# Audio tower, one core: search, token lists and first expert weights drawn into the shared network's loop

## What is computed

```python
scores = jax.nn.softmax(flat_x @ gate_w.T, axis=-1).T
topk_weight, topk_idx = jax.lax.top_k(scores, C)       # C = 752 of 6016, for each of 16 experts
xg = flat_x[topk_idx]
g = jnp.einsum('ecd,eid->eci', xg, Wg)
u = jnp.einsum('ecd,eid->eci', xg, Wu)
h = jax.nn.gelu(g, approximate=False) * u
eo = jnp.einsum('eci,edi->ecd', h, Wd) * topk_weight[..., None]
flat_out = jnp.zeros_like(flat_x).at[topk_idx.reshape(-1)].add(eo.reshape(-1, d))
shared = jax.nn.gelu(hidden @ Sg.T, approximate=False) * (hidden @ Su.T) @ Sd.T
return flat_out + shared
```

## Time and profile before

| | us |
|---|---|
| median of 3 runs | 1786.75 (1784.9 to 1788.12) |
| the profiled execution | 1787.73 |
| its span, first to last instruction | 1785.9 |
| PE busy | 1650.1 (92%) |
| DVE, ACT, POOL busy | 1217.0, 933.1, 1018.6 |
| mean granted clock of PE | 0.961 of full speed |

### The profile page before, as it was taken

The page is one execution under the profiler, slowest core; times in us unless marked ns, Lnnn a source line. Parts: engine busy times, 40 slices in busy tenths (PEclk is TensorE's granted clock), DMA queues, the critical chain, the costliest instruction groups (busy, mean ns, idle before and its releaser), DMA issues.

```text
span 1785.9 us, 47094 instructions
## 1 busy us (share of the span) xinstructions
PE 1650.1 (92%) x15406; PEld 1235.7 (69%) x15406; DVE 1217.0 (68%) x3822; ACT 933.1 (52%) x2157; POOL 1018.6 (57%) x1073
## 2 busy tenths in 40 slices
PE   5983999999999995799998599999999999999997
PEld 5882666777777763577777377777777777777775
DVE  3884889999999995757786555555555555555541
ACT  3553777777777763442335444444444444444432
POOL 3772356666666655722241346676666666666665
PEclk9895999999999997899998699999999999999999
DMA  5542555566666652421001524443333344343322
GB/s 185 162 136 47 122 141 142 141 151 151 151 149 151 145 137 61 129 54 35 28 27 29 176 88 106 107 103 103 100 102 99 87 104 100 88 104 84 99 33 30
DMA packets 173651, 186.81 MB, mean 105 GB/s; under 512 B 119544, under 2 KB 146680, under 8 KB 167416
## 3 DMA queue, kind: packets, MB, share of 16 engines
q1 hardware_dynamic: 138488, 135.03, 26.9%
q0 software_dynamic: 35072, 50.62, 13.9%
HBM read 134.59 MB, written 50.44 MB: 104 GB/s over the span
## 4 chain that ended last, share of the span: by engine, by line
PE 55%; DVE 2%; ACT 1%; DMA 1%; issue 1%; POOL 0%; POOLq 0%; SPq 0%; DVEq 0%
PE psum L1757 28%; PE psum L1774 14%; PE psum L1622 6%; PE psum L1642 4%; PE psum L1737 1%; DMA arena<-e_u 1%; PE psum L1612 0%; PE psum L1682 0%; DVE arena L1228 0%; ACT arena L759 0%; DVE arena L399 0%; PE psum L1653 0%; DVE arena L1173 0%; DVE arena L1306 0%; PE psum L1708 0%
## 5 line engine op out<-in xcount | busy, mean ns | idle before, releaser
L658 POOL TENSOR_TENSOR arena<-arena 128x376 f16<-128x376 f32 x320 | 314.2, 984 | 359.2 <-ACT arena L759 357.7
L1757 PE MATMUL psum<-arena,hidden 128*128 128x376 f16 x3072 | 494.5, 324 | 0.9 <-DVE arena L1370 0.9
L1757 PEld LDWEIGHTS psum<-arena,hidden 128*128 128x128 f16 x3072 | 301.3, 98 | 189.9 <-issue 3.1
L759 ACT ACTIVATE arena<-arena 128x376 f16<-128x376 f32 (+5 forms) x610 | 284.2, 474 | 61.2 <-DVE arena L1306 45.5
L977 ACT ACTIVATE arena<-psum 128x376 f32<-128x376 f32 x256 | 123.7, 483 | 343.6 <-PE psum L1757 343.6
L1133 DVE CUSTOM_DVE_ANT_0 arena<-psum,constants 128x188 f32<-128x188 f32 x768 | 237.3, 346 | 51.4 <-PE psum L1449 41.3
L1380 DVE SCALAR_TENSOR_TENSOR arena<-psum,arena 128x376 f32<-128x376 f32 x256 | 140.6, 549 | 181.0 <-ACT arena L977 179.3
L1774 PE MATMUL psum<-hidden,arena 128*128 128x256 f16 (+1 forms) x2304 | 256.6, 273 | 0.0
L759 ACT ACTIVATE arena<-psum 128x188 f32<-128x188 f32 (+7 forms) x457 | 176.3, 397 | 147.3 <-PE psum L1737 58.0
L1774 PEld LDWEIGHTS psum<-hidden,arena 128*128 128x128 f16 (+1 forms) x2304 | 229.9, 103 | 21.7
L808 ACT ACTIVATE arena<-psum 128x376 f32<-128x376 f32 x384 | 183.8, 480 | 80.5 <-PE psum L1463 78.1
(11 more groups left out here) (159 smaller groups left out, 2736.0 us busy)
## 6 DMA issues: line engine op xcount, KB each, us to landing
arena<-e_g SPq DMA_DIRECT2D x16, 1024.0 KB
arena<-e_u SPq DMA_DIRECT2D x16, 1024.0 KB, 5.0
arena<-e_d SPq DMA_DIRECT2D x16, 1024.0 KB
arena<-x_t SPq DMA_DIRECT2D x32, 376.0 KB, 3.4
weighed<-arena POOLq DMA_DIRECT2D x32, 376.0 KB, 3.9
arena<-q_halves SPq DMA_DIRECT2D x192, 47.0 KB, 3.0
arena<-k_halves SPq DMA_DIRECT2D x96, 94.0 KB, 2.3
arena<-q_halves SPq DMA_DIRECT2D x96, 94.0 KB, 2.2
```

The lines of the kernel that those rows point to most:

```text
L658: nc.gpsimd.tensor_tensor(dst, f, hi, ALU.subtract).then_inc(ready, 1)
L759: return nc.scalar.activation(dst, src, ACT.Copy, scale=scale)
L1757: last = mm(bank[2 * (s % 2) + i][:, 0:CHUNK], w_, a, start=n == 0, stop=n == 5)
```

## The change

It has five parts.

1. The six pieces of work between `above_threshold` and the first `hot_part` stand in steps 45 to 48, not 45 to 51. `HOT` becomes 49, so each `hot_part` stands three steps earlier; 15 of the 16 are in the loop (12 before).
2. `hot_quarter(0)` stands at step 57 and `hot_quarter(1)` at step 61, in the loop. Quarters 2 and 3 stand behind it.
3. At step 62 DVE runs `tokens_of_slots(0)` and lists expert 0 (`FIRST_LISTED`). POOL's gathers of expert 0 wait for this list and stand behind its last low part of the loop. Expert 0's rows lie at another place (`XG[0]`), and their transposes go to PSUM banks 4 and 5.
4. Gate and up weights of expert 0 are loaded in the loop (three transfers at step 40, into the memory of the attention's weights, and one at step 50 into that of the scores). ACT casts them in steps 41 to 46, 51 and 52, twice each: to the fp16 high part, and in place, times 64, in fp32. POOL subtracts the two in steps 50 to 57 (`low_first`, eight subtractions of 128x512).
5. The down weights of expert 0 are cast and subtracted within `expert(0)`: four casts more in ACT's steps 2 to 5, four subtractions more in DVE's steps 3 to 6. `tokens_of_slots(1)` stands behind DVE's product of its step 0, `list_half(1, ...)` in its steps 1 and 2.

```diff
-HOT = FIRST + ROUNDS + 8
+HOT = FIRST + ROUNDS + 5
+FIRST_LISTED = HOT + 13
+LOADS = 40
...
-        XG = [Place(4136)(SLOT_TILES * ROW), at6(SLOT_TILES * ROW)]
+        XG = [Place(prep + 1288)(SLOT_TILES * ROW), at6(SLOT_TILES * ROW)]
...
+        W0 = [v[:, 0:W_GATE].bitcast(F32) for v in (WH, WL)]
+        FIRST_ST = [W0[p // 3][:, p % 3 * 512:(p % 3 + 1) * 512] for p in range(6)] + [PSC[:, p * 512:(p + 1) * 512] for p in range(2)]
...
+        def token_bank(e, c):
+            return bank[(4 if isinstance(e, int) and e == 0 else 6) + c]
...
+                if s == LOADS:
+                    sp.wait_ge(y_added, B)
+                    sp.dma_start(W0[0], e_g[0, :, 0:1536]).then_inc(w_first_in, 16)
+                    sp.dma_start(W0[1][:, 0:512], e_g[0, :, 1536:2048]).then_inc(w_in[0], 16)
+                    sp.dma_start(W0[1][:, 512:1536], e_u[0, :, 0:1024]).then_inc(w_first_in, 16)
+                if s == HOT + 1:
+                    sp.wait_ge(slots, 18)
+                    sp.dma_start(PSC, e_u[0, :, 1024:2048]).then_inc(w_in[1], 16)
...
-            load(0, 0)
             for par in range(2):
                 sp.wait_ge(sh_out[par], 32 * (KS // 2))
-            load(0, 1)
             load(0, 2)
...
+            def low_first(p):
+
+                i, h = divmod(p, 4)
+                pool.wait_ge(sh_added, 2 * 11)
+                pool.wait_ge(wh_ready[i], 2 * h + 2)
+                c = slice(512 * p, 512 * p + 512)
+                nc.gpsimd.tensor_tensor(WEL[0][:, c], FIRST_ST[p], WEH[0][:, c], ALU.subtract).then_inc(wl_ready[i], 1)
...
+                if HOT + 1 <= s < HOT + 9:
+                    low_first(s - HOT - 1)
...
             pool.wait_ge(hl_ready, STEPS)
+            pool.sem_inc(ehl_ready, RING)
+            pool.wait_ge(idx_listed, 4)
             clear_gathered(0)
-            pool.sem_inc(ehl_ready, RING)
             pool.wait_ge(xg_set, 1)
-            pool.wait_ge(idx_listed, 4)
...
+            first_steps = [LOADS + 1 + p for p in range(6)] + [HOT + 2, HOT + 3]
+
+            def high_first(p):
...
+                copy(WEH[0][:, 512 * p:512 * p + 512], FIRST_ST[p], WSCALE).then_inc(wh_ready[i], 1)
+                copy(FIRST_ST[p], FIRST_ST[p], WSCALE).then_inc(wh_ready[i], 1)
...
+                if s in first_steps:
+                    high_first(first_steps.index(s))
                 if s >= HOT + 4:
                     values_of_slots((s - HOT) // 4 - 1, (s - HOT) % 4)
...
+                    if first and 2 <= s < 6:
+                        high_weights(0, 2, s - 2, 0)
...
                 if s == done + 1:
                     above_threshold()
+                    step.mark(nc.vector.tensor_tensor_scan(RANK, ONE, EQ, 0.0, ALU.mult, ALU.add))
                 if s == done + 2:
-                    step.mark(nc.vector.tensor_tensor_scan(RANK, ONE, EQ, 0.0, ALU.mult, ALU.add))
+                    first_of_equal()
+                    ranks_of_hits()
                 if s == done + 3:
-                    first_of_equal()
+                    slots_of_hits()
                 if s == done + 4:
-                    ranks_of_hits()
-                if s == done + 5:
-                    slots_of_hits()
-                if s == done + 6:
                     whole_slots()
-                if s == done + 7:
                     parts_of_slots()
                 if s >= HOT:
                     hot_part(s - HOT)
+                if s == FIRST_LISTED:
+                    tokens_of_slots(0)
+                    list_half(0, (0,))
+            for n in range(STEPS - HOT, 4 * E // QE):
+                hot_part(n)
             down_out(KS - 2, 1)
...
+                    if first and s == 0:
+                        tokens_of_slots(1)
+                    if first and s in (1, 2):
+                        list_half(1, (2 * s - 2, 2 * s - 1))
+                    if first and 3 <= s < 7:
+                        low_expert(0, 2, s - 3, 0)
...
-                if s == done + 5:
+                if s == done + 3:
                     pe.wait_ge(slots, 9)
...
-                if s == done + 6:
+                if s == done + 4:
                     pe.wait_ge(slots, 12)
...
-                if s == HOT + 8:
-                    hot_quarter(0)
+                if s in (HOT + 8, HOT + 12):
+                    hot_quarter((s - HOT) // 4 - 2)
...
-            for q in range(1, E // QE):
+            for q in range(2, E // QE):
                 hot_quarter(q)
...
-            pe.wait_ge(slots, 25)
+            pe.wait_ge(sh_added, 2 * KS)
             token_transposes(0, 0, range(4))
```

46 lines of the change are left out of this document (21 added, 25 removed).

## The result

The changed kernel takes 1793.05 us in the median of 9 runs (1789.19 to 1796.34); the kernel before, run beside it, 1784.70 (9 runs). The ratio is 1.0043, 95% interval 1.003 to 1.0056: **slower by 0.4%**, where 0.3% faster was predicted. The profiled execution of after took 1796.34 us, the longest of its nine, so a part of what its trace shows is the luck of that run; e11 tells which part. Against the forecast of 1780.9 the median is 12.2 us late.

A forecast was written before the change was run, and what follows sets the result against it. PE was taken to set the loop's pace, DVE close behind, then a serial chain. 8.9 won less 2.0 and 1.0 gives 5.9 us off 1787.73, 1781.8; the median lies 1.0 lower: 1780.9, range 1775.5 to 1788.5.

The forecast's parts named there:

- Search: Search drawn together in the loop: ranks end at 906.0, PE waits 2.5 us for the second small product.
- Quarter 0: First quarter in the loop: subtractions cost DVE 0.4 us a step, PE waits 2.4 us (0 to 8).
- rival c: Steps 50 to 55: POOL becomes the bound, PE waits 12.3 us, kernel slower at 1790.8; chance 0.12.
- rival (b): Compares in the loop: DVE pays each subtraction in full, 1.2 us; quarter 0 waits 8.0; 1786.5; chance 0.12.
- Into the tail: From quarter 0 to the last four down blocks: PE waits 3 us for the listing and low part; blocks end 984.9.
- The half clock that I had allowed 1 us for: Last four down blocks behind the loop: a low clock was to cost 1 us (0 to 4.4).
- Quarters 2 and 3: Behind the down blocks: two quarters run back to back in 12.35 us, ending at 997.3.
- Gather, values, transposes: Tail: gathers land 993 to 997.2, values end 989.4, neither late; transposes and splits take 4.95 us as before.
- Expert 0: First steps of expert 0: extra work on DVE and ACT makes PE lose 2 us (0 to 4).
- rival (d): Tail: late gather, late values for quarter 3, or half-clock down blocks cost 3 to 5 us; 1784 to 1786; chance 0.12.
- The main line: Serial chain behind the loop drawn into it: expert 0 starts at 1002.2 in place of 1011.1, 8.9 us won.

The follow-up runs named there:

- e11: The changed kernel as it is, measured and profiled again: 1791.92 us, ratio 1.0023 to the kernel before.
- e7: The changed kernel with the eight subtractions on DVE, in steps 57 and 61, and without ACT's second cast: 1788.66 us, ratio 1.0012.
- e1: The changed kernel with SP's loads behind the loop held until quarter 3 is used: 1786.28 us, ratio 1.0008.
- e3: The changed kernel with POOL's eight subtractions taken out of steps 50 to 57, two ahead of expert 0's gathers, six behind: 1788.27 us, ratio 1.0014.
- e5: The kernel before with only the search's six pieces drawn together into steps 45 to 48: 1790.71 us, ratio 1.0022.
- e10: The kernel before with parts 4 and 5 of the change, the subtractions on DVE and the loads behind the loop held: 1782.40 us, ratio 0.9972.
- e9: The kernel before with six 1 MB copies in device memory added beside quarters 1 and 2: 1794.43 us, ratio 1.0030.
- e12: The changed kernel, search spread one step more, subtractions on DVE, one output piece earlier, loads and last two output transfers held until quarter 3 is used: 1775.89 us, ratio 0.9928.

## Why the prediction was wrong

Expert 0 was predicted at 1002.2, with the 0.65 us by which this trace lies later 1002.85. It started at 1018.7, 15.9 later. This is the account of the one trace, of the longest of nine runs; in e11's expert 0 starts 7.4 us earlier, counted from the start of step 45. The steps, one by one:

- **Search.** Ranks at 906.0: right. The wait: 2.5 predicted, 2.58 in the profile. What the step left out is the clock behind it: behind the wait the granted clock was 0.50 in after (twelve matmuls in 3.78) and 0.58 in e7, and 1.00 in e11, with the groups at 1.93 in e1, e3 and e5 as well. In this trace **3.4 us**, 2.9 of it in the 24 matmuls of the step. The earlier trace rows showed such a fall behind quarter 0; I priced it there and in the tail, and not here.
- **Quarter 0.** With the subtractions 31.3 us from the transposes were predicted and 33.8 measured: **2.5 us**. Without them e3 and e7 gave 28.9, which is the nine steps of PE in the prediction (939.3 - 910.4), while DVE alone was put at 28.5. The price of a subtraction was taken as 0.4 for seven of them, and it is 0.6 or more for eight. POOL did not become the bound (rival c); as a sum rival (b), 1.2 each and a wait of 8.0, was further off than the forecast, but its mechanism is the one that the trace shows. The runs of compares grew by 2.37 and 1.92 us (4.07 against 1.70; 4.16 against 2.24), for 2.8 and 2.3 us of POOL beside them, in which DVE finished three compares (0.14 each from start to start). So where a POOL operation meets the compares DVE pays all of its length but one compare, not half as I took from rows 7; the sum is less than 1.2 each because a part of each subtraction lies beside DVE's product and output piece, which read from PSUM and take 0.55 and 0.68 us there as elsewhere. The Trainium skill ("SBUF — State Buffer", "SBUF: two separate sides") says that the port shared by VectorE and GpSimd is held by one of them for a whole instruction; the trace agrees for DVE, whose compares end 0.08 us behind the POOL operation that they met. Beyond it goes that POOL's low part of 2.24 waited for more than one compare, for the whole run.
- **Into the tail.** Quarter 1 from start to start 20.1 (19.8 predicted), the end of the four down blocks 18.6 behind quarter 1's (18.1 predicted, 2.60 of the 3 us wait for POOL as expected, and 0.84 more for a piece of output, which stands behind 24 compares on DVE). **0.9 us** together. The half clock that I had allowed 1 us for is not in them here; in e11 these 48 matmuls took 7.1 us in place of 5.44.
- **Quarters 2 and 3: the step that failed.** "Two quarters back to back, 12.35" took the duration from a stretch with a DMA share of 0.02 and used it where the share was 0.61. The row that said otherwise was in the same timeline as the earlier trace rows, and I had not taken it in: in quarter 3 of before the last 48 matmuls stand behind a pause of 4.00 us (shown under e10), with a DMA share of 1.03 in it. I took the pauses for part of the matmuls' price without asking what ended them. **9.15 us** in this trace, 3.7 in e11. Of the 9.15, 4.8 are the long pauses, in which PE waits for a packet of its own program that starts late: the packets' times show it in every trace, and traffic alone makes the same pauses in before (e9). 3.3 are the short pauses, whose cause is open, and 1.0 is a lower clock. Holding the loads brings the kernel back to the time of before (e1, 1.0008).
- **Gather, values, transposes.** Right: no wait for either, transposes to expert 0 4.95.
- **Expert 0.** 2 us predicted, 1.0 lost, in waits of 0.16, 0.53 and 0.85 us for DVE's products. The mechanism was right, half the size.

The account closes: 3.4 + 2.5 + 0.9 + 9.15 = 15.95. Of rival (d), "a late link in the tail", I had named the gather, the values and the down blocks; the link that was late was none of these, and its size of 3 to 5 was too small.

The main line, that drawing the chain into the loop wins some 9 us at expert 0's start, is not refuted: e12 has the same quarters and the same list in the loop, and counted from step 45 its expert 0 starts 14.3 us earlier than in before (103.5 against 117.7). But there the subtractions are off POOL, the search has a step more, and loads and outputs wait, and 7.4 of the 14.3 are there in e10 too, without the earlier quarters and list.

Open is what decides whether the clock falls behind a wait of 2.6 us, and what the short pauses around groups of two or three matmuls are. No run tried either by itself. Nor do the traces say when PE's packet was asked for, only when it started.

## What to carry to other kernels

Ask of every pause "issue" in a run of small instructions what it waits for: where it returns at a fixed count of instructions, look in the instruction queue for the packet that ends just ahead of the engine's next instruction. Its start can be put off by the transfers beside it, and the run's duration then holds only for traffic like that in which it was measured. When work is moved earlier, look at what the transfers behind it then collide with; holding the loads that are not yet needed made nothing late here and won 3 to 6 us (e1). Where DVE is near 93% busy in a run of compares, a POOL operation beside it is paid for by DVE almost in full.
